# The second layer's bias on TensorE during the sort, and the net turned at the end of a step

## The reference, cut to what matters

```python
edge_sum = jax.ops.segment_sum(edge_attr, src, num_segments=50000)
inputs = jnp.concatenate([x, edge_sum], axis=1)      # 50000 x 256
h = jax.nn.elu(inputs @ W0 + b0)                     # W0 256 x 128
h = jax.nn.elu(h @ W2 + b2)                          # W2 128 x 128
out = h @ W3 + b3                                    # W3 128 x 128
x = _layernorm(x + out)
```

## Time and profile before

| | us |
|---|---|
| median of 3 runs | 547.99 |
| lowest and highest run | 544.12, 551.29 |
| the profiled execution, its own time | 546.7 |
| its span, first to last instruction | 544.9 |
| TensorE busy | 507.9 |
| VectorE busy | 459.7 |
| ScalarE busy | 418.9 |
| GpSimd busy | 371.8 |

### The profile page before, as it was taken

How to read it: one execution, slowest core, us unless ns; L and a number is a source line. 1 busy time by engine, 2 the same in 40 slices (tenths; PEclk the granted TensorE clock), 3 DMA queues, 4 the chain that set the end, 5 groups by cost and what they waited for, 6 DMA issues and landing times.

```text
span 544.9 us, 10037 instructions
## 1 busy us (share of the span) xinstructions
PE 507.9 (93%) x2881; PEld 362.2 (66%) x2881; DVE 459.7 (84%) x1216; ACT 418.9 (77%) x1534; POOL 371.8 (68%) x311
## 2 busy tenths in 40 slices
PE   6898999879979999999999999999999999999980
PEld 4465656556656767777777777777777777777670
DVE  7999888878989988898898888887889888888781
ACT  4888778768877888778777777787877877877770
POOL 6877777778742787777887777777677443333355
PEclk9999999999999999999999999999999999999995
DMA  5678989888767997776666766454445443332122
GB/s 162 183 200 252 270 278 277 249 242 249 220 196 214 262 273 212 206 207 183 184 184 181 196 187 175 132 149 135 125 135 150 122 134 117 96 101 91 55 79 53
DMA packets 87756, 96.98 MB, mean 178 GB/s; under 512 B 26403, under 2 KB 56595, under 8 KB 87703
## 3 DMA queue, kind: packets, MB, share of 16 engines
q1 hardware_dynamic: 58375, 70.67, 41.5%
q0 software_dynamic: 28896, 25.29, 19.0%
q10 hardware_dynamic: 432, 0.39, 0.3%
HBM read 58.10 MB, written 45.04 MB: 189 GB/s over the span
## 4 chain that ended last, share of the span: by engine, by line
PE 72%; DMA 10%; DVE 7%; ACT 5%; issue 3%; POOLq 1%; POOL 1%; SPq 1%
PE z_ps L663 16%; PE z_ps L664 16%; PE l_ps L617 15%; PE l_ps L653 15%; DMA x_sb<-x_items_dram 7%; PE side_ps L579 4%; PE l_ps L628 4%; ACT sq L760 2%; PE side_ps L645 2%; DVE h L1025 1%; DMA words<-word_rows_dram 1%; DVE e L1023 1%; DMA word_rows_dram<-net 1%; DVE o_sb L1056 1%; POOLq L475 1%
## 5 line engine op out<-in xcount | busy, mean ns | idle before, releaser
L663 PE MATMUL z_ps<-center,xT 128*128 128x128 f32 (+1 forms) x986 | 190.4, 275 | 1.3 <-ACT xT L731 1.3
L664 PE MATMUL z_ps<-w3c,h 128*128 128x128 f32 (+1 forms) x986 | 190.1, 275 | 0.0
L663 PEld LDWEIGHTS z_ps<-center,xT 128*128 128x128 f32 (+1 forms) x986 | 154.8, 191 | 43.2 <-issue 38.7
L487 POOL DMA_INDIRECT out_dram<-pair_edge,target_i x100 | 120.9, 1209 | 89.6 <-issue 84.9
L760 ACT ACTIVATE sq<-z_ps 128x128 f32<-128x128 f32 (+1 forms) x493 | 129.3, 278 | 67.7 <-PE z_ps L664 67.2
L468 POOL DMA_INDIRECT pair_edge<-pairs_dram,edge_i x100 | 124.6, 1246 | 45.8 <-issue 30.2
L664 PEld LDWEIGHTS z_ps<-w3c,h 128*128 128x128 f32 (+1 forms) x986 | 149.0, 191 | 0.0
L458 POOL DMA_INDIRECT x_early<-in_x_dram,src_i x100 | 122.9, 1229 | 32.8 <-issue 29.6
L653 PE MATMUL l_ps<-h,w 128*128 128x512 f32 (+1 forms) x248 | 128.3, 599 | 1.0 <-DVE h L1025 1.0
L738 ACT ACTIVATE e<-l_ps,bias 128x512 f32<-128x512 f32 (+1 forms) x150 | 102.2, 682 | 21.3 <-PE l_ps L653 14.8
L1025 DVE SCALAR_TENSOR_TENSOR h<-l_ps,neg_bias,e 128x512 f32<-128x512 f32 (+1 forms) x150 | 111.1, 741 | 5.3
(11 more groups left out here) (144 smaller groups left out, 445.2 us busy)
## 6 DMA issues: line engine op xcount, KB each, us to landing
out_dram<-o_sb SPq DMA_DIRECT2D x98, 256.0 KB, 4.0
x_sb<-x_items_dram SPq DMA_DIRECT2D x97, 256.0 KB, 4.4
pairs_dram<-x_early SPq DMA_DIRECT2D x25, 250.0 KB
keyB<-key_rows_dram SPq DMA_DIRECT2D x25, 250.0 KB, 4.3
pairs_dram<-in_edge_attr_dram SPq DMA_DIRECT2D x24, 256.0 KB
x_early<-in_x_dram,src_i POOLq DMA_INDIRECT x100, 5.4
pair_edge<-pairs_dram,edge_i POOLq DMA_INDIRECT x100, 4.5
out_dram<-pair_edge,target_i POOLq DMA_INDIRECT x100
```

The lines of the kernel that those rows point to most:

```text
L487: nc.gpsimd.indirect_dma_start(out=out[:, :], out_offset=bass.IndirectOffsetOnAxis(ap=target_i[0:EP, c:c + 1], axis=0), in_=pair_edge[0:EP ...
L663: T.matmul(z, xT[:, c % X, j * q:(j + 1) * q], center[:], start=True, stop=False)
L664: mm = T.matmul(z, h2[:, c % H, j * q:(j + 1) * q], w3c[:], start=False, stop=True)
```

## The change

In steps 8 to 34 the second layer takes the one-step form too. TensorE's `layer2` adds a three-row bf16 product behind its matmul, ScalarE's exponential gets the bias -1 in place of `bias2`, and VectorE does one operation in place of two. For that the second layer's bias plus 1 is split and turned as well: the splits lie in VectorE's steps 1 to 4, the transpose in TensorE's step 5, the copy (two sets of rows) in VectorE's step 6. And TensorE does `turn_net` after layer 3 of its step in place of after layer 2.

```diff
-        bias_parts = sb("bias_parts", [P, 3])
-        bias_rows = sb("bias_rows", [P, P], BF16)
+        bias_parts = sb("bias_parts", [P, 2, 3])
+        bias_rows = sb("bias_rows", [P, 2, P], BF16)
...
+        def fused2(s):
+            return FUSED_FROM <= s < KEY_AT
...
             def turn_b0():
-                pe.wait_ge(parts_split, 1)
-                T.transpose(z_ps[2][0:3, P:2 * P], bias_parts[:], ident[:]).then_inc(setup_mm, 1)
+                pe.wait_ge(parts_split, 2)
+                for layer in range(2):
+                    mm = T.transpose(z_ps[2][0:3, (layer + 1) * P:(layer + 2) * P], bias_parts[:, layer, :], ident[:])
+                mm.then_inc(setup_mm, 1)
...
-            def add_bias(ps, n, done):
-                T.matmul(ps, bias_rows[0:3, :], ones_row[0:3, 0:n], start=False, stop=True).then_inc(done, 1)
+            def add_bias(layer, ps, n, done):
+                T.matmul(ps, bias_rows[0:3, layer, :], ones_row[0:3, 0:n], start=False, stop=True).then_inc(done, 1)
...
-            def layer2(c):
+            def layer2(s, c):
...
-                T.matmul(l2_ps[c % 2][:, 0:n], w2[:], h1[:, c % H, 0:n], start=True, stop=True).then_inc(l2_ready, 1)
+                ps = l2_ps[c % 2][:, 0:n]
+                mm = T.matmul(ps, w2[:], h1[:, c % H, 0:n], start=True, stop=not fused2(s))
+                if fused2(s):
+                    add_bias(1, ps, n, l2_ready)
+                else:
+                    mm.then_inc(l2_ready, 1)
...
-                    beside = [lambda: None, lambda: turn_net(TURNED.index(c - SORT_AT))]
+                    beside = [lambda: None, lambda: None, lambda: turn_net(TURNED.index(c - SORT_AT))]
...
-                    parts.append(lambda: exp(c - 3, l2_ps[(c - 3) % 2], l2_ready, bias2, e2, exp2_ready))
+                    parts.append(lambda: exp(c - 3, l2_ps[(c - 3) % 2], l2_ready, minus_one if fused2(c) else bias2, e2, exp2_ready))
...
-            def split_b0(part):
+            def split_bias(layer, part):
+                if (layer, part) == (1, 0):
+                    link(V.tensor_scalar(bias_rest[:], bias2[:], 1.0, None, ALU.add))
...
-                V.tensor_copy(bias_rows[0:3, :], z_ps[2][0:3, P:2 * P]).then_inc(bias_rows_ready, 1)
+                V.tensor_copy(bias_rows[0:3, :, :], z_ps[2][0:3, P:3 * P].rearrange("p (l f) -> p l f", l=2)).then_inc(bias_rows_ready, 1)
...
-                        elu(False, c - 3, l2_ps[(c - 3) % 2], bias2, neg_bias2, e2, exp2_ready, min2_ready, h2, h2_ready)
+                        elu(fused2(c), c - 3, l2_ps[(c - 3) % 2], bias2, neg_bias2, e2, exp2_ready, min2_ready, h2, h2_ready)
...
-                    parts = [make_bias_x, first_layer, lambda: split_b0(0), second_layer]
-                elif c in (2, 3):
-                    parts = [lambda: split_b0(c - 1), first_layer, output, second_layer]
+                    parts = [make_bias_x, first_layer, lambda: split_bias(0, 0), second_layer]
+                elif c == 2:
+                    parts = [lambda: split_bias(0, 1), first_layer, lambda: split_bias(0, 2), second_layer]
+                elif c == 3:
+                    parts = [lambda: split_bias(1, 0), first_layer, lambda: split_bias(1, 1), second_layer]
+                elif c == 4:
+                    parts = [lambda: split_bias(1, 2), first_layer, output, second_layer]
```

More of the change, by code:

```diff
@@ L620, in layer1 @@
                 elif is_dense(c):
-                    add_bias(ps, n, l1_ready)
+                    add_bias(0, ps, n, l1_ready)
                 elif c == LAST:
@@ L681, in _ @@
                 if item_in(c - 3):
-                    parts.append(lambda: layer2(c - 3))
+                    parts.append(lambda: layer2(c, c - 3))
                 if item_in(c - 5):
@@ L855, in make_bias_x @@
                 V.tensor_copy(bias_x[:], z_ps[1][:, 0:1]).then_inc(bias_x_ready, 1)
-            def split_b0(part):
+            def split_bias(layer, part):
+                if (layer, part) == (1, 0):
+                    link(V.tensor_scalar(bias_rest[:], bias2[:], 1.0, None, ALU.add))
                 link(V.tensor_copy(bias_low[:], bias_rest[:]))
                 if part < 2:
-                    link(V.tensor_copy(bias_parts[:, part:part + 1], bias_low[:]))
-                    link(V.tensor_tensor(bias_rest[:], bias_rest[:], bias_parts[:, part:part + 1], ALU.subtract))
+                    link(V.tensor_copy(bias_parts[:, layer, part:part + 1], bias_low[:]))
+                    link(V.tensor_tensor(bias_rest[:], bias_rest[:], bias_parts[:, layer, part:part + 1], ALU.subtract))
                 else:
-                    V.tensor_copy(bias_parts[:, part:part + 1], bias_low[:]).then_inc(parts_split, 1)
+                    V.tensor_copy(bias_parts[:, layer, part:part + 1], bias_low[:]).then_inc(parts_split, 1)
             def make_bias1():
```

## The result

| | kernel before | changed kernel |
|---|---|---|
| median of 12 runs each, us | 545.12 | 548.87 |
| lowest and highest | 540.63, 551.29 | 546.50, 552.37 |
| profiled execution, us (its span) | 546.7 (544.9) | 547.9 (546.1) |

Ratio 1.0078, 95% interval 1.0051 to 1.0105: the change costs 0.8%, 2.8 to 5.7 us of 545. The same two kernels on another occasion gave 548.76 against 544.37 us, ratio 1.0091 (1.0061 to 1.0122). Ratios leave out slow runs, those over 1.5% above the fastest of their kernel, which medians hold, so a ratio can differ a little from that of the medians beside it.

The account below looks back on a forecast made before the run. TensorE, VectorE and the DMA queue were near their limits. Products' 14.0 and start's 1.7 us, mostly absorbed by waits, left 0 to 3.3 us; +1.5, taken between, on 547.99 gave 549.5 us, range 544.5 to 556.5.

Parts of the forecast that it names:

- rival 2: Up to the words: cost partly absorbed, VectorE late with output or last compares; +3.5 to +8 us, 551.5 to 556; chance 0.23.
- the late turn: Net turned after layer 3, 14 times: VectorE's output just fits, cost nothing; the sort's tail may make words 0 to 1.5 us late.
- VectorE's relief: Steps 8 to 34: one operation for two saves 0.58 us 27 times, 15.7 us of VectorE, going into waiting.
- rival 4: VectorE paces the sort, so its freed 15.7 us would bring a gain of over 11 us; chance 0.02.
- The product at 0.52 us: TensorE, steps 8 to 34: 0.32 us per product plus 0.20 on the next matmul, 27 times, 14.0 us.
- Rival 1: Product costs only 0.22 to 0.32 us; 5.8 to 8.6 us added fits within the waits, 545 to 548 us; chance 0.18.
- The start: Second bias split on VectorE before TensorE's step 7: 1.57 us plus up to 0.1 for the copy; step 7 1.7 us late.
- rival 3: In the sort, x loads follow the engines, so DMA waits stay; +12.4 us, 560.4 us; chance 0.07.
- the words' way in the sum: Shift at the words' turn (162.72 us): 0 to 3.3 us from TensorE, 0 to 1.5 from the sort; +1.5 taken.

Follow-up runs that it names:

- Relief alone: Kernel before with the one-operation form for the second layer in steps 8 to 34, that layer's bias left out, no product; ratio 1.0026.
- products alone: Kernel before with one three-row product of zeros added to the second layer in each of steps 8 to 34; 549.70 against 548.05 us, ratio 1.0048.
- second split alone: Changed kernel without products, one-operation form and late turn, leaving second bias split, transpose and wider copy; ratio 1.0019 against the kernel before.
- spread and later: Kernel before with attribute transfers spread over steps 2 to 38 and the bias-row wait moved ahead of step 7's layer 3; ratio 1.0001.
- changed kernel with the later wait: Changed kernel with TensorE's bias-row wait moved from step 7's start to ahead of its layer 3; ratios 0.9986 (slower chip) and 1.0077 against kernel before.
- three products each: Kernel before with three products of zero rows after each second-layer matmul in steps 8 to 34, 81 in all; ratio 1.0216 in four runs.
- kernel before with the later wait: Kernel before with TensorE's bias-row wait moved from step 7's start to ahead of its layer 3; ratio 0.9985 on the slower chip.

## Why the prediction was right, and where it was mis-sized

**The forecast held** (549.5, range 544.5 to 556.5 us; measured 548.87), and its direction, a small loss. The shift was +1.5 us; the profiled executions give 1.2, the medians 3.75. That the absolute time came so close has a share of luck: I added 1.5 us to 547.99, a median of three runs; twelve runs gave 545.12. By the shift alone, 3.75 us is the low end of rival 2 (+3.5 to +8 us). Its mechanism, a VectorE made late by the late turn, isn't what the runs show; that all slack is used up at the words and VectorE passes the rest on is nearer to it than my sum was.

**VectorE's relief** was right in size (15.7; 15.9 with the split, 16.3 alone) and in place: into waits. Relief alone, 1.0026, shows that VectorE wasn't the pacer (rival 4).

**The product at 0.52 us** was right, for the untried neighbour too. TensorE's steps came out as summed: 29.59 to 34.13, 4.54 us with both products, and 3.51 + 0.52 = 4.03 and 4.01 (34.13 to 38.14) with one. Rival 1, the cheap product, is out: 0.215 us holds only behind another such product.

**The start** was 1.4 us longer against 1.7 forecast; that step 7 began at 26.02 and not at 27.3 us is because VectorE's setup in that execution ran 1.1 us earlier (bias_x at 8.21 against 9.27 us). Most of what the forecast missed at later steps is this: step 14 came at 55.6 us (57.0 forecast), step 29 at 120.8 (122.4), the turn of the words at 160.9 (162.6).

**That loads don't follow TensorE** (against rival 3, and the waits view's reading) is shown: the load of step 12 left at 53.43 us before, 53.42 changed, and a later one at 92.04 and 92.07, while TensorE was 1.3 to 2.6 us later in between; from 102 to 133 us the loads even go out 1.5 to 2.5 us earlier than before. The loads have some play of their own: in products alone these two went out at 54.07 and 93.68 us. Why the queue has this pace I had wrong, or at least open: it isn't the attribute transfers. Each slow load between 39 and 122 us stands behind a transfer of gathered rows, and those leave every 6.7 us on average from 39.5 to 119.4 us, near the 6.1 us in which GpSimd issues their four gathers (one each 1.52 us). But one leaves in two of three steps, so 6.7 us is also just one and a half steps at the pace that TensorE had. No run changed the gathers' pace, so this stays open.

**The step that was mis-sized is the words' way in the sum.** I took 0 to 3.3 us there from TensorE's lateness alone against its 3.29 us wait, and 0 to 1.5 from the last compare. Neither bound: the last compare ran at 148.29 us (150.1 to 150.5 forecast), the queue was free, the store left at 148.53 us (150 to 152 forecast), and TensorE turned the words at 160.90 us without a wait, 1.8 us earlier than before. But the time wasn't won, since the next in line was VectorE: it came to the words at 162.95 us (before 163.10). I hadn't costed the steps 35 to 38, in which VectorE has the two-operation form in both layers and works 13.58 of 14 us. The stretch from 149 to 163 us, changed and second split alone:

```profile
149.00:163.00 14.00, 14.00 (x82) 10.01 (x81) 13.58 (x30) 12.57 (x49) 6.76 (x6) 1.00 0.78 237
```

```profile
149.00:163.00 14.00, 12.43 (x72) 8.95 (x71) 12.61 (x35) 11.56 (x42) 6.74 (x6) 1.00 0.82 235
```

From step 35 on VectorE can't catch up: from TensorE's start of step 35 to VectorE's operation on the words it takes 16.0 to 16.4 us in all four executions with the 27 products and the wait at its old place. So the time at which TensorE hands it step 35 goes through to the words and on to step 42. In relief alone, second split alone and spread and later step 35 is at 141.9 to 144.3 us, VectorE would be ready at 157.9 to 160.1 us, the queue brings the words so that it begins on them at 160.4 to 160.8 us, and step 42 begins at 173.1 to 173.8 us. With the products, in four executions of three kernels, it is 146.7 to 147.2, 163.0 to 163.2 and 175.9 to 177.5 us. That is 2 to 4 us, about the 3.75 and 4.39 us of the medians; in three of the four up to 1.4 us of it is the lower clock in step 41. This is read from traces: no run made steps 35 to 38 cheaper for VectorE. In the changed kernel with the later wait it doesn't hold, since there the queue stored the words late. And of the 1.2 us between the two profiled executions only 0.2 is there at step 42; 0.7 more comes at step 49 and the rest later, unexplained.

**And the execution that I argued from was a late one** (1.6 us above the median of twelve). Its loads held step 35 to 145.2 us, and its words were turned at 162.72 us, 2.3 to 2.7 us later than in the three kernels just named. I had called the words' way fixed from the store on. It isn't: from store to turn it takes 12.5 us there and 9.7 us in second split alone, though both store at 150.3 to 150.4 us. The reload of the words held the queue 2.58 us in the kernel before and 0.30 us in the other:

```profile
155.72 2.58 SPq L419 DMA_DIRECT2D words<-word_rows_dram  x1
```

```profile
156.54 0.30 SPq L424 DMA_DIRECT2D words<-word_rows_dram  x1
```

Against this execution the change looks like +0.2 us at step 42, against the three kernels 2 to 4 us. That an ordinary execution of the kernel before looks like those three is my inference; it has one trace only. Waits of one execution were taken as slack that is always there.

**The late turn** costs nothing that can be measured (-0.5 to +0.3%), as forecast, though not because it just fits: alone it makes TensorE wait 8.4 us ahead of layer 3, 4.2 of it for VectorE's outputs, and 8.0 us of load waits go.

How much of the 0.8% is the products' is known only to the interval of products alone (0.05 to 0.9%); that the rest is the start (second split alone: -0.2 to +0.6%) fits the numbers but isn't resolved. That products cost time at all rests mainly on two results, this one and the three products each.

## What to carry to other kernels

When three engines and a queue are all near their limit, moving work from the one with no waits behind it to the one that the others wait for was no gain here even where waits took most of it: price it by the successor's slowdown too, 0.52 us here for a product of 0.32. Slack read from one execution's DMA waits must be checked in a second one before it is spent. And when a wait disappears, follow the next engine in line past the edit's own steps: here it was VectorE in the four steps after the last one that had been made cheaper.

## What the runs showed of the hardware

A 3-row bf16 product of 512 columns costs 0.52 us between float32 matmuls, 0.215 us behind another of its kind. The 215.7 ns that the Trainium skill gives for back-to-back matmuls (page "TensorE: Matmul & The Clock Gate", section "Wait — 56ns, not 53.3ns?") would, taken as the price in both places, be borne out by the trace in the second only. Behind TensorE's waits of 2.9 to 3.8 us the granted clock fell to the lower level for some microseconds in five executions, and stayed at 1.00 behind waits of 3.3 us in the first profiles of before and of the changed kernel. One chip of three ran the same kernel 5% slower (573.95 us), and not by its clock: between 300 and 400 us, at a granted clock of 1.00, TensorE was busy for 87.82 us in the kernel before with the later wait there, against 99.88 of 100 us in the first profile of before. Each engine has idle times of up to 2.4 to 3.9 us there that the waits view puts down to no instruction of this core. They come in bursts: between 400 and 500 us TensorE was busy throughout on that chip too. From that kernel's table of stretches:

```profile
300.00:400.00 100.00, 87.82 (x496) 62.15 (x496) 72.64 (x164) 67.45 (x249) 76.93 (x65) 1.00 0.50 143
```
